# A four-layer transformer kernel: a new order of steps around the routed experts, writes of results moved to another queue, and register loads moved behind a wait

## The chip, the cores and the metric

The kernel runs on one core of a Trainium2 chip. A core has five engines that run their own instruction streams: TensorE (PE in the profile, with its weight loads as PEld), VectorE (DVE), ScalarE (ACT), GpSimd (POOL) and SyncE (SP). They meet at semaphores, and sixteen DMA engines move data for them. The metric is the time of one execution on the device, in microseconds.

## The reference

Sixteen blocks of 128 rows with 256 features go through four layers; each layer is a cross attention and a feed-forward part, each behind a LayerNorm and added to x:

```
x = x + L0_xattn(ln(x), ctx); x = x + L0_ffn(ln(x))
x = x + L1_xattn(ln(x), ctx); x = x + L1_ffn(ln(x))     # L1_ffn: routed experts
x = x + L2_xattn(ln(x), ctx); x = x + L2_ffn(ln(x))
x = x + L3_xattn(ln(x), ctx); x = x + L3_ffn(ln(x))
```

The change lies around L1_ffn, in which each row goes to two of seven experts and to one shared expert:

```
gate = xt @ Wr + br
_, ids = top_k(gate + gate_bias, 2)
probs  = softmax(gate where chosen, else -inf)
u  = xt @ Wup[e] + bup[e]                     # per expert e
g  = silu(u @ Wgate[e] + bgate[e]) * u
eo = g @ Wdown[e] + bdown[e]
out = sum_e probs[:, e] * eo[e]
su = xt @ Wsu + bsu;  sg = silu(su @ Wsg + bsg) * su
out = out + sg @ Wsd + bsd
```

and its follower L2_xattn, with 16 heads of 16 features, a LayerNorm over each head's queries and keys, and 16 further context rows with projections of their own. All of it is fp32 in and out.

## The kernel before

**Stages.** The program numbers its stages: 0 and 1 are layer 0, 2 is L1_xattn, 3 the router of L1_ffn, 8 its routed tiles, 9 its shared expert with the gathering and combining of results, 4 and 5 layer 2, 6 and 7 layer 3. x stays in SBUF through the whole program; each stage runs over 16 blocks of 128 rows.

**The order.** Each engine walks through a string of letters (`ORDER`, one string each for T = PE, V = DVE, A = ACT, G = POOL). A letter stands for one step of a stage (`STEPS` names the steps and the engines that take part), and `timetable()` gives each letter's next occurrence the next block. So the strings alone decide what stands behind what on an engine. A step waits on semaphores for its inputs and for its PSUM bank; a wait that an engine has passed once is not repeated. SP has no string: it issues weights and tiles in the order of its code.

**Router (3).** Per block: `lnA`, `lnB`, `xT` (normalise, transpose), `r1` (scores on PE, top two on DVE, exponential on ACT), `r2` (weights of the two), `pT`, `acc`, `rk` (running counts), `sc` (POOL scatters the block's normalised rows into the DRAM buffer `rows_in`, sorted by expert). After the last block `tab` makes the table of 38 tiles: first row and expert of each.

**Tiles (8).** For tile t, SP reads its first row into a register and loads 128 rows (`tile_in`, six buffers). Step `cp` reads the tile's expert number into a register (`value_load`, on ACT at L1440 and on DVE at L2009) and copies that expert's weights from the SBUF block that holds all of them into one of two buffers: ACT the up matrix, DVE gate and down (L2012). PE then transposes (`tT`, L1088), and multiplies with up (L1096), gate (L1105) and down (L1112, L1113). DVE adds biases and multiplies by u (L2019, L2024), ACT does the activation and evicts the result into one of three buffers. POOL writes it to the DRAM buffer `rows_out` (L2362).

**Shared expert and combination (9).** Steps `up`, `ga`, `dn` on PE (L1123, L1131, L1138) run for the 16 blocks; they stand in the order among the router's steps, the tiles and the start of stage 4. When all of `rows_out` is written, POOL gathers per block two sets of rows (`gt`, two indirect DMAs at L2356, ring of six buffers), and DVE adds them to x with their weights (`cmb`, L2048 and L2050). A block's `cmb` must be done before its `lnA` of stage 4, in which POOL takes a part (L2269).

**Stage 4.** Its weights come by eleven DMAs (L711 to L722). `cw` (DVE, L1624 to L1666, once) subtracts head means from them. PE's first step is `vp`, the values of the context (L851); it waits for `cw` and for stage 4's `init` on POOL.

## Time and profile before

| | us |
|---|---|
| median of three runs | 2449.25 |
| the three runs | 2446.4, 2449.25, 2453.49 |
| profiled execution | 2446.4 |
| its span | 2444.5 |
| PE busy | 2304.7 (94%) |
| DVE busy | 1689.5 (69%) |
| ACT busy | 1178.2 (48%) |
| POOL busy | 444.0 (18%) |

The span runs from the first instruction to the last; the device's time is 1.9 us more. "Busy" is the time in which an engine executes; waiting at a semaphore isn't counted. In timelines a bracket behind an instruction gives how long its engine had been idle, and what released it.

The stretches of this case within the span: PE's last output projection of stage 2 ends at 1107.3, the first tile's transpose starts at 1145.9, the last tile's down ends at 1273.3, stage 4's `vp` starts at 1287.7 and its first score matmul at 1304.7, and its last output ends at 1537.4.

### The profile page before, as it was taken

The page shows a single profiled execution, that of the slowest core. Times are in us where ns is not written, and L with a number is a line of the kernel's source. Part 1 is how long each engine was busy: PE and PEld are TensorE (multiplying, and loading weights), DVE is VectorE, ACT ScalarE, POOL GpSimd, SP SyncE. Part 2 cuts the span into 40 slices and gives each one's busy share as a digit, 9 for nine tenths or more (in the row PEclk, how much of TensorE's full clock was granted, in tenths as well). Part 3 has the DMA queues.
Part 4 walks back from the last instruction along what each step waited for, and adds up shares of the span by engine and source line. Part 5 has one row for each costly group of instructions (what it writes and reads, how often), then busy time and mean ns, then how long its engine had stood idle before and what let it go on. Part 6 is the DMA issues. An engine that isn't in the chain of part 4 may idle for free.

```text
span 2444.5 us, 43996 instructions
## 1 busy us (share of the span) xinstructions
PE 2304.7 (94%) x16327; PEld 1811.9 (74%) x16327; DVE 1689.5 (69%) x4612; ACT 1178.2 (48%) x3093; POOL 444.0 (18%) x514
## 2 busy tenths in 40 slices
PE   4899999999999999997998999999999999999987
PEld 3666999999888888886997887886666666665554
DVE  5997887876355555546447888326776777869997
ACT  3677877677433333332643444114555555553211
POOL 2220100000011111002127842001222222220000
PEclk9999999999999999998998999999999999999999
DMA  9200300000210000002211110301000000000000
GB/s 342 68 2 2 104 1 1 1 1 1 80 33 10 10 9 10 10 9 65 83 61 29 34 36 1 121 1 52 1 1 1 1 1 1 1 1 3 13 9 11
DMA packets 52976, 74.88 MB, mean 31 GB/s; under 512 B 4666, under 2 KB 45644, under 8 KB 51740
## 3 DMA queue, kind: packets, MB, share of 16 engines
q1 hardware_dynamic: 47868, 58.69, 7.3%
q0 software_dynamic: 4896, 13.38, 1.7%
q8 instruction: 131, 2.15, 0.4%
q14 instruction: 81, 0.66, 0.1%
HBM read 45.32 MB, written 26.74 MB: 29 GB/s over the span
## 4 chain that ended last, share of the span: by engine, by line
PE 68%; DVE 18%; ACT 7%; issue 4%; POOL 2%; SPq 1%; DMA 0%; POOLq 0%; DVEq 0%; ACTq 0%
PE pb L972 5%; PE pb L1041 5%; PE pb L964 4%; PE pb L978 4%; PE pb L885 4%; PE pb L1156 4%; PE pb L1010 4%; ACT workA L1525 3%; PE pb L1033 3%; PE pb L911 2%; PE pb L1021 2%; PE pb L1164 2%; PE pb L1227 1%; PE pb L1096 1%; ACT workA L1420 1%
## 5 line engine op out<-in xcount | busy, mean ns | idle before, releaser
L2269 POOL TENSOR_TENSOR sm<-sm,neghalf 128x1 f32<-128x1 f32 x128 | 72.8, 569 | 1047.2 <-DVE sm L1603 1047.0
L1390 ACT ACTIVATE areaB<-i128h,workB 128x128 f16<-128x128 f16 x512 | 156.2, 393 | 4.3 <-DVE workB L1828 4.2
L1525 ACT ACTIVATE workA<-pb,workA 128x128 f32<-128x128 f32 x256 | 114.0, 457 | 81.6 <-DVE workA L2137 81.6
L1618 DVE TENSOR_TENSOR x<-x,pb 128x256 f32<-128x256 f32 x112 | 46.8, 418 | 137.5 <-PE pb L1164 53.4
L1347 ACT ACTIVATE areaA<-pb 128x512 f32<-128x512 f32 x192 | 105.3, 600 | 62.9 <-PE pb L885 62.6
L885 PE MATMUL pb<-workA 32*128 32x128 f16 (+2 forms) x2048 | 121.7, 256 | 14.1 <-DVE workA L1713 4.6
L1227 PE MATMUL pb<-areaA,workA 128*128 128x256 f32 x512 | 122.7, 383 | 10.6 <-DVE workA L2149 9.9
L885 PEld LDWEIGHTS pb<-workA 32*128 32x128 f16 (+2 forms) x2048 | 92.4, 144 | 47.8 <-issue 27.6
L1010 PE MATMUL pb<-xT,areaA 128*128 128x128 f32 x1024 | 125.1, 279 | 0.0
L1010 PEld LDWEIGHTS pb<-xT,areaA 128*128 128x128 f32 x1024 | 122.6, 196 | 2.0 <-issue 1.3
L964 PE MATMUL pb<-areaB 128*128 128x128 f32 x1024 | 123.4, 277 | 0.6 <-ACT workB L1380 0.6
L1227 PEld LDWEIGHTS pb<-areaA,workA 128*128 128x128 f32 x512 | 94.5, 191 | 35.3 <-issue 12.1
L1041 PE MATMUL pb<-areaA,workA 128*128 128x256 f32 x512 | 120.0, 381 | 0.0
L964 PEld LDWEIGHTS pb<-areaB 128*128 128x128 f32 x1024 | 118.1, 192 | 1.6 <-ACT workB L1380 0.8
L2338 POOL TENSOR_TENSOR workA<-workA,neghalf 128x4 f32<-128x4 f32 x64 | 64.5, 1010 | 270.0 <-DVE workA L2116 270.0
L978 PE MATMUL pb<-areaB,workB 128*128 128x256 f32 x512 | 113.5, 380 | 0.0
L1041 PEld LDWEIGHTS pb<-areaA,workA 128*128 128x128 f32 x512 | 94.4, 190 | 17.4 <-issue 6.7
L1420 ACT ACTIVATE workA<-pb,workA 128x128 f32<-128x128 f32 x256 | 90.6, 369 | 32.0 <-DVE workA L1860 28.7
L978 PEld LDWEIGHTS pb<-areaB,workB 128*128 128x128 f32 x512 | 96.1, 190 | 13.0 <-issue 0.5
L1156 PE MATMUL pb<-workB,areaB 128*128 128x128 f32 (+1 forms) x768 | 97.6, 280 | 0.0
L1412 ACT COPY workA<-pb 128x512 f32<-128x512 f32 x64 | 38.0, 594 | 122.8 <-PE pb L1010 122.7
L1156 PEld LDWEIGHTS pb<-workB,areaB 128*128 128x128 f32 (+1 forms) x768 | 86.6, 179 | 10.1 <-issue 5.8
(412 smaller groups left out, 5915.9 us busy)
## 6 DMA issues: line engine op xcount, KB each, us to landing
rows_in<-areaB SPq DMA_DIRECT2D x7, 2048.0 KB, 17.5
areaA<-rows_in SPq DMA_DIRECT2D x38, 128.0 KB, 2.0
rows_out<-areaA POOLq DMA_DIRECT2D x38, 128.0 KB, 2.0
areaA<-in_L_xattn_Wo SPq DMA_DIRECT2D x2, 2048.0 KB, 19.4
areaB<-in_edT SPq DMA_DIRECT2D x1, 2048.0 KB, 9.5
areaB<-in_L_ffn_e_up SPq DMA_DIRECT2D x1, 2048.0 KB, 15.5
areaA<-in_wq1T SPq DMA_DIRECT2D x1, 2048.0 KB, 8.3
areaA<-in_L_xattn_Wq SPq DMA_DIRECT2D x1, 2048.0 KB, 7.6
```

Source lines behind the costliest of these rows:

```text
L885: m = eng.matmul(p[i][:, j * 128:(j + 1) * 128], one, two, start=True, stop=True)
L964: m = eng.matmul(p[:, e * 128:(e + 1) * 128], w.ed[:, k, (4 * c + e) * 128:(4 * c + e + 1) * 128], xT[:, k, :], start=(k == 0), stop=(k == 1))
L972: m = eng.matmul(p[:, g * 64:(g + 1) * 64], u.B[c % 2][:, g, :], u.Am[c % 2][:, g, :], start=True, stop=True)
L978: m = eng.matmul(p[:, 0:256], G[:, e, :], w.eu[:, e, :], start=(e == 0), stop=(e == 15))
L1010: m = eng.matmul(p[:, h * 128:(h + 1) * 128], w.wq[:, 4 * c + h, k], xT[:, k, :], start=(k == 0), stop=(k == 1))
L1041: m = eng.matmul(p[:, 0:256], u.OT[i][:, h], w.wo[:, 4 * c + h], start=(c == 0 and h == 0), stop=(c == 3 and h == 3))
L1156: m = eng.matmul(p[0:M, m_ * 128:(m_ + 1) * 128], wm[:, k, mt * 128:mt * 128 + M], xT[:, k, :], start=(k == 0), stop=(k == 1))
L1227: m = eng.matmul(p[:, 0:256], u.OT[i][:, h], w.wo[:, 4 * c + h], start=(c == 0 and h == 0), stop=(c == 3 and h == 3))
L1347: eng.activation(u.P[n % RP], bank(s, tag, b, c // 2)[:, :], ACT.Exp, scale=1.0 / math.sqrt(hd)).then_inc(freed(s, tag, b, c // 2)[0], 1)
L1390: m = eng.activation(u.far[:, g], i128h[:, :], ACT.Square, bias=u.at[b % 2][:, 1, 8 * c + g:8 * c + g + 1])
L1420: m = eng.activation(u.P[i][:, h], p[:, h * 128:(h + 1) * 128], ACT.Exp, accum_out=u.den[i][:, h:h + 1], bias=u.nm[i][:, h:h + 1])
L1525: m = eng.activation(u.P[i][:, h], p[:, h * 128:(h + 1) * 128], ACT.Exp, accum_out=u.den[i][:, h:h + 1], bias=u.nb[i][:, h:h + 1], scale=u ...
```

## The change

Four things are edited.

1. The four order strings, from the end of stage 1's and stage 2's work to stage 4, and a pair of letters in stage 6 (T and V).
2. The writes of `rows_out` go from POOL to SP: step `dn` of stage 8 loses its "G", POOL's function `tiles` goes, and SP's loop gets `tile_out`.
3. Stage 4's weights (eleven DMAs) are issued behind the load of tile 6, no longer ahead of the tiles.
4. In `cp`, on ACT and DVE, `value_load` stands behind the wait for the end of the tile two earlier.

```diff
@@ STEPS
-    8: (("cp", 1, "AV"), ("tT", 1, "TA"), ("up", 1, "TV"), ("ga", 1, "TAV"), ("dn", 1, "TAG")),
+    8: (("cp", 1, "AV"), ("tT", 1, "TA"), ("up", 1, "TV"), ("ga", 1, "TAV"), ("dn", 1, "TA")),
@@ ORDER, one line of "V" out of some hundred changed ones
-        "eafhOkgkbekhkfgkkefhkkrgkkihkkQgrakkbihQkkatbQkkaQkkbeifarrbeQQfQQgeathfigkkberkkfrgrahtbhikkrQekkftgrkkirkkhtgrkkre"
+        "QQieafbiQeafQgebfhakgkbekkhfagkkefhbkkrgkkiahkkbQekgkfrikkrhagbtFhkkiekkfrekkfirgktkrarrgbeFFhfrkthtkrkkirergtkhkfta"
@@ SP
+            def tile_out(t):
+                d.wait_ge(*freed(8, "dn", t))
+                eng.dma_start(rows_out[128 * t:128 * (t + 1), :], u8.y[t % 3]).then_inc(S[f"m_y{t % 3}"], 16)
+
             def tiles():
                 for b in range(NB - 4, NB):
                     d.wait_ge(*scattered(b))
                 d.wait_ge(S["m_tab"], 1)
-                for t in range(TILES):
-                    tile_in(t)
+                for t in range(TILES + 8):
+                    if t < TILES:
+                        tile_in(t)
+                    if t == 6:
+                        weights(4)
+                    if t >= 8:
+                        tile_out(t - 8)
@@
             for k in range(FIRST + 1, LAST + 1):
-                weights(k)
                 if k == 4:
                     tiles()
+                else:
+                    weights(k)
@@ ACT, cp
                     a.wait_ge(S["m_tab"], 1)
-                    e = eng.value_load(u3.tei[0:1, b:b + 1], min_val=0, max_val=EXPERTS - 1)
                     if b >= 2:
                         a.wait_ge(*full(8, "u", b - 2))
+                    e = eng.value_load(u3.tei[0:1, b:b + 1], min_val=0, max_val=EXPERTS - 1)
                     eng.copy(u.w[b % 2][:, 0:1], w3.all[:, bass.ds(e, 1), 0]).then_inc(S["m_wa"], 1)
@@ DVE, cp
                     v.wait_ge(S["m_tab"], 2)
-                    e = eng.value_load(u3.tei[0:1, b:b + 1], min_val=0, max_val=EXPERTS - 1)
                     if b >= 2:
                         v.wait_ge(*full(8, "dn", b - 2))
+                    e = eng.value_load(u3.tei[0:1, b:b + 1], min_val=0, max_val=EXPERTS - 1)
                     eng.tensor_copy(u.w[b % 2][:, 1:3].unsqueeze(1), w3.all[:, bass.ds(e, 1), 1:3]).then_inc(S["m_wv"], 1)
@@ POOL
-            def tiles(step, b, c):
-                g.wait_ge(*freed(8, "dn", b))
-                eng.dma_start(rows_out[128 * b:128 * (b + 1), :], u8.y[b % 3]).then_inc(S[f"m_y{b % 3}"], 16)
```

Lines of the new kernel lie ten further than those of the old one from stage 0's code on, and 12 further for `cp` on DVE before its wait. What the new strings do is seen in the instructions, below; "waits" names the semaphores.

**First place: DVE, block 15 of the router, between the max subtraction and the softmax sum.** Before, `cw` stands there (L1624 to L1666, areaA is stage 4's weights):

```order
L1909 TENSOR_SCALAR workB<-workB 128x7 [waits dve_own]
L1624 TENSOR_REDUCE areaA<-areaA 128x32 [waits w_in4]
L1626 TENSOR_SCALAR areaA<-areaA 128x32 [waits dve_own]
L1628 TENSOR_TENSOR areaA<-areaA 128x512 [waits dve_own]
...
L1666 TENSOR_SCALAR areaA<-areaA,cst 128x256 x2
L1912 TENSOR_REDUCE workB<-workB 128x1 [waits m_exp]
L1914 RECIPROCAL workB<-workB 128x1 [waits dve_own]
```

Now the same place has one multiplication of the shared expert (L2049):

```order
L1919 TENSOR_SCALAR workB<-workB 128x7 [waits dve_own]
L2049 TENSOR_TENSOR workB<-workB 128x256 [waits bank_free4]
L1922 TENSOR_REDUCE workB<-workB 128x1 [waits m_exp]
L1924 RECIPROCAL workB<-workB 128x1 [waits dve_own]
L1928 MEMSET workB 128x1 [waits dve_own]
```

`cw`, sixteen instructions, has left the router.

**Second place: DVE in the tiles.** bank_full5 and 6 are PSUM banks that PE fills with down's result; bank_full1 to 4 those of up and gate. Before, the register load (TENSOR_LOAD and two ISA instructions) is ahead of the wait for down:

```order
L2024 TENSOR_TENSOR areaA<-areaA 128x256 [waits bank_free3,bank_free1]
L2009 TENSOR_LOAD workB
L2009 ISA x2
L2012 ISA [waits bank_full6]
L2012 COPY areaA<-areaB 128x1024
```

Now the wait stands on the load:

```order
L2034 TENSOR_TENSOR areaA<-areaA 128x256 [waits bank_free4,bank_free2]
L2029 TENSOR_TENSOR areaA<-pb,workB 128x256 [waits m_gm,bank_full4,bank_full1]
L2021 TENSOR_LOAD workB [waits bank_full6]
L2021 ISA x2
L2022 ISA
L2022 COPY areaA<-areaB 128x1024
```

The load, its two register instructions and the copy are all behind down's end now.

**Third place: PE in the tiles, as it is now.** L1098 and L1099 are the transpose, L1106 up, L1115 gate, L1122 and L1123 down:

```order
L1122 MATMUL pb<-areaA 128x256 [waits bank_free5,m_gm]
L1123 MATMUL pb<-areaA 128x256
L1098 MATMUL pb<-cst,areaA 128x128 [waits bank_free0,m_x1]
L1099 MATMUL pb<-cst,areaA 128x128
L1106 MATMUL pb<-areaA 128x128 [waits bank_free2,m_wa]
L1106 MATMUL pb<-areaA 128x128 x3
L1115 MATMUL pb<-areaA 128x128 [waits bank_free3,m_wv]
L1115 MATMUL pb<-areaA 128x128 x3
```

m_wv is DVE's copy of gate and down; here it waits for the down that stands at the head of these rows, and a transpose and an up lie between.

**Fourth place: DVE ahead of stage 4, as it is now.** m_g3 to m_g5 and m_g0 are the gathers of a block; L2058 and L2060 are `cmb`:

```order
L2058 SCALAR_TENSOR_TENSOR x<-areaA,workB,x 128x256 [waits bank_free6,m_g4]
L2060 SCALAR_TENSOR_TENSOR x<-areaA,workB,x 128x256 [waits dve_own]
L1634 TENSOR_REDUCE areaA<-areaA 128x32 [waits w_in4]
...
L1676 TENSOR_SCALAR areaA<-areaA,cst 128x256 x2
L2058 SCALAR_TENSOR_TENSOR x<-areaA,workB,x 128x256 [waits bank_free7,m_g5]
L2060 SCALAR_TENSOR_TENSOR x<-areaA,workB,x 128x256 [waits dve_own]
L2058 SCALAR_TENSOR_TENSOR x<-workB,x 128x256 [waits bank_free6,m_g0]
L2060 SCALAR_TENSOR_TENSOR x<-workB,x 128x256 [waits dve_own]
L1735 SCALAR_TENSOR_TENSOR workA<-pb,cst,areaA 128x16x16 [waits bank_full0,l2_init]
```

The first pair is block 10's. Before, two combinations stood ahead of stage 4's first eviction (L1725) beyond block 0's, and `cw` none.

**POOL.** Before, three blocks are gathered, and the others between stage 4's steps. Now POOL's part is:

```order
L2366 DMA workB<-rows_out,workB 128x256 [waits m_y2,m_out,m_y1,m_y0]
L2366 DMA workB<-rows_out,workB 128x256 x5
L2279 TENSOR_TENSOR sm<-sm,neghalf 128x1 [waits ln_var0]
L2366 DMA areaA<-rows_out,workB 128x256 x2
L2279 TENSOR_TENSOR sm<-sm,neghalf 128x1 [waits ln_var0]
L2366 DMA areaA<-rows_out,workB 128x256 x2
```

This goes on to block 5 with one L2279 per block (four in all), and then without one to block 11: 22 gathers for blocks 0 to 10. The shared expert's steps for blocks 9 to 15 stand behind the last tile on PE, with the down steps of blocks 8 to 15.

## Rows read from the trace of the kernel before

**Rows 1.** The page, section 1: busy us (share of the span) xinstructions.
```profile
PE 2304.7 (94%) x16327; PEld 1811.9 (74%) x16327; DVE 1689.5 (69%) x4612; ACT 1178.2 (48%) x3093; POOL 444.0 (18%) x514
```

**Rows 2.** Stretches: length, busy us of each engine (xcount), clock, DMA share, GB/s.
```profile
1107.30:1145.90 38.60, 24.41 (x163) 21.25 (x161) 26.39 (x89) 9.94 (x21) 9.81 (x18) 0.84 0.19 52
1145.90:1273.30 127.40, 125.08 (x902) 116.17 (x903) 61.48 (x133) 71.83 (x193) 20.05 (x37) 0.98 0.24 77
1273.30:1287.70 14.40, 12.94 (x103) 12.25 (x101) 9.05 (x25) 3.77 (x12) 9.41 (x12) 1.00 0.26 82
1287.70:1304.70 17.00, 13.46 (x68) 10.33 (x68) 14.96 (x39) 4.29 (x9) 15.83 (x12) 1.00 0.08 25
1304.70:1537.40 232.70, 224.14 (x2231) 187.48 (x2232) 187.29 (x526) 97.99 (x178) 120.41 (x78) 0.96 0.08 23
```

**Rows 3.** PE timeline: start, us, instruction, [idle before <-releaser].
```profile
1131.02 0.80 PE L1138 MATMUL pb<-areaB,workB 128*128 128x256 f32 x1 [6.45 <-DVE workB L2039]
...
1137.53 0.39 PE L1081 MATMUL pb<-workB,cst 128*128 128x8 f32 x2
...
1145.90 0.47 PE L1088 MATMUL pb<-cst,areaA 128*128 128x128 f32 x1 [6.91 <-DMA areaA<-rows_in]
```

**Rows 4.** DVE timeline, router block 15; columns as in rows 3.
```profile
1122.84 0.68 DVE L1624 TENSOR_REDUCE areaA<-areaA 128x32 f32<-128x512 f32 x1
...
1129.60 0.15 DVE L1912 TENSOR_REDUCE workB<-workB 128x1 f32<-128x7 f32 x1
```

**Rows 5.** PE timeline, two tiles in the middle of the tile stage.
```profile
1184.31 0.60 PE L1112 MATMUL pb<-areaA 128*128 128x256 f32 x2
...
1185.18 0.27 PE L1088 MATMUL pb<-cst,areaA 128*128 128x128 f32 x1
...
1185.40 1.06 PE L1096 MATMUL pb<-areaA 128*128 128x128 f32 x8
1186.29 1.11 PE L1105 MATMUL pb<-areaA 128*128 128x128 f32 x8
```

**Rows 6.** DVE timeline there: the copy of a tile's gate and down weights.
```profile
1185.50 0.69 DVE L2012 COPY areaA<-areaB 128x1024 f32 x1 [2.04 <-PE pb L1113]
```

**Rows 7.** Line 2009: durations ns min/median/max, first and last start.
```profile
L2009 DVEq TENSOR_LOAD <-workB x38: 297/304/544, 1147.8 to 1266.1; - x38
...
L2009 DVEq SEQ_ASSERT  x38: 23/23/35, 1148.7 to 1266.7; - x38
```

**Rows 8.** POOL timeline, the last write of results and the first gathers.
```profile
1274.04 0.54 POOL L2362 DMA_DIRECT2D rows_out<-areaA  x1 [1.19 <-ACT areaA L1464]
1276.80 1.02 POOL L2356 DMA_INDIRECT workB<-rows_out,workB  x1 [2.21 <-DMA rows_out<-areaA]
1278.12 0.97 POOL L2356 DMA_INDIRECT workB<-rows_out,workB  x1 [0.30 <-issue]
...
1283.16 0.95 POOL L2356 DMA_INDIRECT workB<-rows_out,workB  x1 [0.30 <-issue]
...
1285.00 1.11 POOL L2356 DMA_INDIRECT areaA<-rows_out,workB  x1 [0.19 <-issue]
```

**Rows 9.** The page, section 6: KB each, us from issue to landing.
```profile
areaA<-rows_in SPq DMA_DIRECT2D x38, 128.0 KB, 2.0
```

**Rows 10.** SP timeline: first and last of eleven weight issues, first tile loads.
```profile
1107.97 0.37 SPq L711 DMA_DIRECT2D areaA<-in_L_xattn_Wq  x1
...
1112.73 0.42 SPq L722 DMA_DIRECT2D areaA<-in_nwc  x1
1143.93 1.49 SPq L764 DMA_DIRECT2D areaA<-rows_in  x2
```

**Rows 11.** DVE timeline, the combination of block 0 and what follows.
```profile
1280.86 0.49 DVE L2048 SCALAR_TENSOR_TENSOR x<-workB,x 128x256 f32<-128x256 f32 x1 [0.87 <-DMA workB<-rows_out,workB]
...
1281.90 0.43 DVE L1599 BATCH_NORM_STATS2 sm<-x 128x6 f32<-128x256 f32 x1
```

**Rows 12.** PE timeline, the first step of stage 4.
```profile
1287.74 0.67 PE L851 MATMUL pb<-areaA,ctxT 128*128 128x256 f32 x2 [0.57 <-POOL workA L2308]
```

More of the change, by code:

```diff
@@ L83 @@
[L83 to L86 removed]
+        "nnnkhplrnhnlsnhlnnpnjhlnrnksplnCnlnDplnnCElrnnFpslnnnDnFpCFrEsFDNFNCEFDNFENFFNFNPNNFFkPkNNFkNFCNFDNFCENFDNFCEDNEkPkN"
@@ new lines @@
+        "NkFFkFPkNNFlFNCNDFCEFDFCENNPNNPFFFDNNFCENNFFFPDNNFCENNFFFPDNNFCENNFFFPDNNFCENNFFFPDNNFCENNFFFPDNNFCENNcFFFPDcNENlNcF"
+        "FNlFlFPNNlFNFNlFlFPNlNFNmFNFPNNdPeddeegdcdheegidhegidhegidhecigddheCgiDhegdFhGegHihiigdcheCgihDgihgFdGhHeiigdheCiDdg"
+        "dFhGeHeicgdhegihdiegdheCgihDgihdFiGeHdcdeegddheecigddheCgiDhegdFhGegHihiigdcheCgihDgihgFdGhHeiigdheCiDdgdFhGeHeicgdh"
+        "egihdiegdheCgihDgihdFiGeHdcdeegddheecigddheCgiDhegdFhGegHihiigdcheCgihDgihgFdGhHeiigdheCiDdgdFhGeHeicgdhegihdiegdheC"
@@ new lines @@
+        "gihDgihdFiGeHdcdeegddheeigddheCgiDhegdFhGegHihiigddheeCgiDhgdiFhGeHgihgdheigdheCgihDgihiFiGMHMNNMOONCMODNMMONFNFGOHM"
+        "OJNbbcbcbbddceebcdcbdebccdebcbcdbecbedbcdebcOdbecedbcdebcdbecedbcdebcdbecedcbdecbdebcdecbdecbdebcdcecbdebdbecdecbdec"
+        "bdbecdecbdecbdbecdecbdecbdecdecdedeMMdeNNdeOeMONMMONNMOMONcNMMcNNcOOOOidcidcdhcdjjchljmdoomhojoqcljimhojomdoojlqcqmi"
+        "jmsholooomtooimhjdqqjoodcjslqimjtoomlFqFFFFqdmhoooosmsqoojthtqqcjiqdsjlthsmtoomijqdjoojlcqmiloomshqmoodtmijhcdjqoooo"
@@ new lines @@
+        "NNGHIMNMNPJKGOOHIJMMNNOOPKBMNMNABABGOOHAIMMNNOOJPKMNMNGHIPJOOKBMNMNOOABMNMNGHIOOJPKMNMNOOABMNMNGHIOOJPKMNMNOOABMNMNG"
+        "HIOOJPKMNMNOOABMNMNGHIOOJPKMNMNOOAaBMNMNGHIOOJPKbiiiMNMNOOMNaMNGHIOOJPKbaMNObMNOaMNGHMNIJOOKbPMNMNOOMNMNOOPMNOMNOMNm"
+        "MNOOPOOPefeeffabheefhefhefhaebiiiiABfhefDhEeFfhGeHfhiiiiABafhebfhDEhFGhHefiiiiABhefDEFhGeHefafbhefhiiiiAeBfhefhDEhFG"
+        "eHafbeeffheaebiiiiABfhefDhEeFfhGeHfhiiiiABafhebfhDEhFGhHefiiiiABhefDEFhGeHefafbhefhiiiiAeBfhefhDEhFGeHafbeeffheaebii"
@@ L2373, in gpsimd_program @@
                     experts(step, b, c)
-                elif s == 8:
-                    tiles(step, b, c)
                 elif s == 2:
```

63 lines of the change are left out of this document (25 added, 38 removed).

## The prediction

> **What bounds the kernel now.** I read the page's first line first [rows 1]: TensorE (PE) is busy 94% of the span, VectorE (DVE) 69%. So a change pays only where PE idles, and costs wherever it makes PE wait. The table of stretches comes next [rows 2]: the five stretches in which the order changes. PE is busy 24.4 of 38.6 us between the last output projection of stage 2 and the first expert tile, 125.1 of 127.4 in the tiles, 12.9 of 14.4 and 13.5 of 17.0 at the handoff to stage 4, and 224.1 of 232.7 in stage 4 itself. Only the first has much to win. PE's timeline there [rows 3] has two long holes: 6.45 us before 1131.02 and 6.91 before 1145.90. I count from the profiled execution: 2446.4 us, of which 2444.5 is the span and 1.9 lies around it. The median of the three runs is 2449.25, 2.85 higher.
>
> **The change, part by part.**
>
> *Router tail.* The first hole ends on a DVE step queued behind `cw`, the centring of stage 4's weights. It runs from 1122.84 to the next reduce at 1129.60 [rows 4]: 6.8 us, and the product that PE waits for (L2039) comes behind both. In the new order `cw` isn't in that chain, and the product (L2049) directly follows the max subtraction. So the route table is ready 6.8 us sooner. The second hole stays: from the table's matmul at 1137.53 to the first tile's transpose at 1145.90 are 8.4 us of DVE, SP and DMA chain, and PE has as little to fill it with. Value: -7. Bounds: 0 (another input is late there) and -13.4 (both holes, 6.45 + 6.91).
>
> *Tiles.* PE needs per tile 0.22 (transpose), 0.89 (up), 0.89 (gate, as many matmuls) and 0.87 (down), from the differences of the starts in [rows 5]: 2.87, or 109.1 for 38. The other shared-expert work in the stretch was ten steps of 0.88, 8.8; now six, 5.3: -3.5, which comes back after the tiles. The order now has two shapes. Weight buffers are two, so gate(b) waits for DVE's copy(b), and that for the end of down(b-2). Before, the copy starts at 1185.50 and takes 0.69 [rows 6], and gate starts at 1186.29, 1.11 after down gave way at 1185.18 [rows 5]: the 0.22 + 0.89 of other PE work between them just hides it. Now the register load of the expert number comes behind that wait. It is a load (0.30), register arithmetic and a check (0.02) [rows 7]; from the load's last start (1266.1) to the check's (1266.7) it is 0.6. Before, it ran while DVE waited (the copies' engine waits for down, 2.04 us in [rows 6]). So the need grows from 1.11 to 1.7. In the new order, PE's work between down(b-2) and gate(b) is 1.11 for 14 tiles, 0.89 for five, 0.22 and 0 for one each; the others have 1.76 or more. Stalls: 14 x 0.6 + 5 x 0.8 + 1.5 + 1.7 = 15.6, of which 12.6 (21 x 0.6) is the moved load and 3 the tighter order. Before, the stretch took 127.4 for 117.9 of work (109.1 + 8.8); of these 9.5 I let 3 go, as the new order leaves gate and down further apart where they stood close. Stage: -3.5 + 15.6 - 3 = +9. Bounds: -3.5 if the load costs nothing (-3.5 + 3 - 3), +15 if every tile with 1.76 also stalls by 0.35. I take +9, since in [rows 5, 6] copy and gate touch without a gap (1185.50 + 0.69 is 1186.19, gate starts 0.10 later).
>
> The Trainium skill ("DMA: Bandwidth & Descriptors", section "Latency and other measured facts") gives a register load a floor of about 600 ns; [rows 7] has 297 to 304, so the trace doesn't agree. By the page each of the 21 stalls would be 0.3 longer, the sum 6 us higher.
>
> *Writes from SP.* The 38 writes of results leave POOL and stand on SP, tile t-8's behind the load of tile t. POOL spent 0.54 on each [rows 8] and was otherwise idle (20.0 of 127.4 busy), so nothing comes back there. A load now waits behind a write of eight tiles earlier, which is long evicted. A load of the same size from SP lands 2.0 after its issue [rows 9]; from POOL's last write to the first gather it was 2.76 (1274.04 to 1276.80, [rows 8]), landing and the gather's own start. So the first gather stays about as far behind the last tile. Value 0, bounds -0.5 and +3.
>
> *Weights of stage 4.* Eleven issues, from 1107.97 to the end at 1113.15 [rows 10], 5.2 us, now stand between the loads of tiles 6 and 7. Load 6 is issued once tile 0 is transposed; from there 0.75 for it (two loads took 1.49), 5.2, 0.75 for load 7 and 2.0 to landing are 8.7, and a few us more behind the weights' own data. Tile 7 is due on PE 7 x 2.87 = 20 us after tile 0, or 16 as transposes run ahead. 0, bounds 0 and +2.
>
> *Handoff.* This is the term that decides. PE's first step of stage 4 (vp, L861) waits for `cw`, which on DVE stands behind the combination of block 10, and that for the 22nd gather. Gathers follow each other by 1.25 to 1.32 us (1276.80 to 1278.12, 1.32, [rows 8]; most later ones at 1.25); one with a LayerNorm helper in between takes 1.84 (1283.16 to 1285.00), 0.6 more. From the first gather: 21 x 1.26 + 4 x 0.6 = 28.9 to the start of the 22nd; 2.74 from a block's last gather to its combination (1278.12 to 1280.86, [rows 8, 11]); 1.0 for its two operations (to 1281.90); 6.8 for `cw`; 0.2 to PE. Sum 39.6. The first gather starts 3.4 after the last tile (1273.3 in [rows 2], 1276.80), so vp starts 43.0 after the tiles; before 14.4 (1273.3 to 1287.74, [rows 2, 12]). +28.6. PE has 22 shared steps x 0.88 = 19.4 to fill it with, and then stands still for about 20 us. Bounds: +22 (helpers free, `cw` half as long) and +31.
>
> *Stage 4.* Before, 17.0 + 232.7 = 249.7 from vp to its last output [rows 2]. In the 17.0, the first LayerNorm and transposes are late; now x and xn of four blocks are ready: -2.3, and 1.7 more since qk of a block is done sooner. Ten combinations of 1.0 and four LayerNorm halves (some 3 us) leave DVE's part in the stage, and the gathers POOL's. DVE had 187.3 busy of 232.7, PE 224.1, so it was not DVE that filled the stage; what can come back is PE's 8.6 idle us, and I take 6. Sum -10. Bounds 0 and -19 (every microsecond of DVE counts).
>
> Sum: -7 + 9 + 28.6 - 10 = +20.6, on the profiled execution 2467.0, against the median 2469.8. A check by PE's idle time: -6.5 in the router, +12.6 in tiles, about +20 in the handoff (43.0 - 19.4 less the 5.0 idle of before [rows 2] gives 18.6), -4 to -6 in stage 4: +19 to +21.
>
> **The rivals.**
>
> *A, the forecast*: +20.6, 2469.8.
>
> *B, no change.* The load in the tile loop hides after all (DVE's instruction stream reads it ahead of the wait, or PE has more slack than its starts show), -12, and stage 4 gives 7 more because combinations no longer sit in its DVE chains. 20.6 - 19 = +1.6, 2451. For it: DVE was 80% busy in stage 4 (187.3 of 232.7) with long chains. Against: a register load written behind a wait runs behind it, and PE's slack is one of 8.6 us.
>
> *C, faster.* DVE, not PE, paces all of these stages. Then all 19 us of DVE work that leave stage 4 come back rather than 10 (-9), the tile load hides (-12), both router holes go (-6.4), and the helpers among the gathers cost nothing (-2.4): 20.6 - 29.8 = -9, 2440. For it: PE at 94% [rows 1] is a busy share, and waits of under 0.1 between its instructions would not show in it. Against: PE's starts follow each other without a gap in [rows 5]. It decides from 20 us of gain outside the handoff on.
>
> *D, worse.* The tile loop is set by the copies: ScalarE's copy of up(b) has its load moved behind a wait in the same way, and a stalled gate delays gate's activation, down and so the next copy. 0.35 more on each of 38 tiles (+13): 2483. For it: ACT is busy 71.8 of 127.4 only, but in the chain of each tile. Against: up(b) has a whole gate and down ahead of it. That the writes on SP hold up loads would be of the same size.
>
> That the change doesn't do what it says would be B's first half alone: +8, inside A's range.
>
> **How the numbers follow.** A 0.72, B 0.08, C 0.07, D 0.13. A's own range: terms' bounds about half used, 2457 to 2482. The whole range reaches down to B and up to D: 2450 to 2486. About 0.3% (7.3 us) is what a measurement of this kernel tells from no change: faster (C) 0.07, same (B and the low end of A) 0.09, slower 0.84.
>
> **What would show it.** The first tile's transpose about 7 us earlier than 1145.90, with no `cw` on DVE before it. In the tiles, PE idle of some 13 us in pieces of 0.6 to 0.8 before L1115, released by DVE's copy L2022, whose start trails down's end by 0.6 more. A hole of about 20 us on PE before L861, with DVE waiting for gathers, 22 of them before `cw`, and a lower granted clock just behind it. Stage 4 shorter by about 10. The forecast is wrong if that hole is under 10 us, if L2022's load is not in the path, or if stage 4 shortens by over 15.

## The result and the profile after

The changed kernel takes 2489.48 us (median of four runs, 2486.1 to 2492.1), the kernel before 2449.9 beside it: 39.6 us more, a ratio of 1.0161 with a 95% interval of 1.0141 to 1.0180. It is slower, as forecast, but by nearly twice the forecast 20.6, and lies above the range that was given (2450 to 2486).

The profiled execution took 2500.7, 11 above the median, with a mean granted clock of 0.975 where the other four had 0.977 to 0.981. So its stages add up to +54.3 against the profiled execution before, not to +39.6; where that matters it is said. Every length of a stage below is from one profiled execution. Page, section 1, of the changed kernel (against [rows 1]):

```profile
PE 2320.0 (93%) x16327; PEld 1815.3 (73%) x16327; DVE 1694.9 (68%) x4612; ACT 1178.0 (47%) x3095; POOL 425.3 (17%) x476
```

The same stretches as in [rows 2], and stage 2 ahead of them (length, busy us of each engine, clock, DMA share, GB/s):

```profile
640.00:1097.10 457.10, 455.56 (x2868) 372.39 (x2867) 238.51 (x764) 175.17 (x683) 45.58 (x55) 1.00 0.07 23
1097.10:1131.00 33.90, 24.21 (x168) 21.27 (x167) 21.29 (x79) 9.83 (x21) 11.22 (x20) 0.97 0.06 20
1131.00:1280.40 149.40, 128.85 (x878) 113.78 (x879) 60.72 (x129) 67.51 (x191) 0.00 (x0) 0.97 0.25 77
1280.40:1328.00 47.60, 21.66 (x150) 18.93 (x148) 32.22 (x77) 5.75 (x18) 34.02 (x40) 0.81 0.27 80
1328.00:1591.70 263.70, 250.68 (x2285) 206.70 (x2286) 190.34 (x533) 104.23 (x185) 111.46 (x60) 0.91 0.04 11
```

Stage 2 of the kernel before, which I had not looked at:

```profile
640.00:1107.50 467.50, 466.57 (x2859) 382.63 (x2858) 236.63 (x765) 171.12 (x665) 45.33 (x57) 0.97 0.07 23
```

The span less PE's busy time grew from 139.8 to 178.9 us. From the landmarks on PE (profiled executions, us):

| part | before | after | difference | forecast |
|---|---|---|---|---|
| to the end of stage 2 | 1107.5 | 1097.1 | -10.4 | 0 |
| to the first tile | 38.4 | 33.9 | -4.5 | -7 |
| tiles | 127.4 | 149.4 | +22.0 | +9 |
| last tile to vp | 14.4 | 47.7 | +33.3 | +28.6 |
| vp to stage 4's last output | 249.6 | 263.7 | +14.1 | -10 |
| stages 5 to 7 | 904.5 | 904.5 | 0 | 0 |

The end of stage 2 is measured from the span's start. Counted from the first of the router's score products, which stand among stage 2's steps (687.4 before, 690.0 after), to the stage's end, it is 420.1 before and 407.1 after, 13.0 less; 12 of these are the time at half clock, 27 us before and 3.4 after (from the granted clock in steps of 2 us), and the rest is a little less work between the two marks.

Every part but the last is off: the first was not in the forecast, stage 4 has the wrong sign, and the tiles and the handoff lie above their bounds (+15 and +31). The hole in front of vp is there as forecast, 21 us. The other stretches had to be taken apart by experiments.

In the tiles, two groups of the changed kernel hold nearly all of PE's waits (gate, and the transposes; busy us, mean ns, idle before <-releasers):

```profile
L1115 PE MATMUL pb<-areaA 128*128 128x128 f32 x304 | 42.2, 283 | 5.7 <-DVE areaA L2022 5.6
...
L1098 PE MATMUL pb<-cst,areaA 128*128 128x128 f32 x38 | 12.2, 322 | 20.7 <-DMA areaA<-rows_in 17.7 <-ACT areaA L1458 2.8
```

and the same two before:

```profile
L1105 PE MATMUL pb<-areaA 128*128 128x128 f32 x304 | 40.6, 277 | 0.0
...
L1088 PE MATMUL pb<-cst,areaA 128*128 128x128 f32 x38 | 11.3, 298 | 8.8 <-DMA areaA<-rows_in 7.5 <-ACT areaA L1448 1.1
```

The transposes waited 17.7 us for their loads, the gates 5.6 for DVE's copy. Of the 17.7, 6.8 lie ahead of the first tile and so outside the stage (6.9 of the 7.5 before); within the stage the waits for loads are 10.9 us against 0.6. I had put 15.6 on the copy and nothing on the loads. How a load comes to be late shows in three timelines of one tile. ScalarE's eviction of a down result (L1474) stands behind a weight copy (L1453) that waits for a later tile's up:

```profile
1199.03 0.62 ACT L1453 COPY areaA<-areaB 128x512 f32 x1 [2.24 <-PE pb L1106]
1199.56 0.36 ACT L1474 COPY areaA<-pb 128x256 f32<-128x256 f32 x1
```

SP waits for that eviction with the write (L768), and the load of tile 24 (L764) stands behind the write; the load ahead of it had been issued six us before:

```profile
1194.92 0.34 SPq L764 DMA_DIRECT2D areaA<-rows_in  x1
1199.95 0.33 SPq L768 DMA_DIRECT2D rows_out<-areaA  x1
1201.04 0.34 SPq L764 DMA_DIRECT2D areaA<-rows_in  x1
```

PE gets the tile 2.9 us after the issue:

```profile
1203.91 0.33 PE L1098 MATMUL pb<-cst,areaA 128*128 128x128 f32 x1 [1.85 <-DMA areaA<-rows_in]
```

Before, an eviction was done 1.4 to 1.5 us after the start of its down, in all 38 tiles; in the changed kernel it is some 4 to 10 us from the tenth tile to about the thirtieth. Before, loads were issued 12 to 21 us ahead of their transposes from tile 8 on; in the changed kernel it is 2.0 to 4 us from tile 15 on. The queue's own waits say the same, total us, times and longest:

```profile
SPq L768 <- ACT areaA L1474: 89.4, 33, 6.7
```

Before, SP waited in the tiles only for the buffers of its loads.

### The profile page after: what moved, and what is told of

Read it like the earlier page. It is cut to its first block, busy times and chain, and to the rows that moved or that the text cites. A ratio compares the mean times of both kernels' runs of the same rounds, so it can differ in the third digit from the quotient of the medians.

```text
span 2498.9 us, 43992 instructions
## 1 busy us (share of the span) xinstructions
PE 2320.0 (93%) x16327; PEld 1815.3 (73%) x16327; DVE 1694.9 (68%) x4612; ACT 1178.0 (47%) x3095; POOL 425.3 (17%) x476
## 4 chain that ended last, share of the span: by engine, by line
PE 67%; DVE 18%; ACT 6%; issue 4%; POOL 2%; DMA 2%; SPq 1%; ACTq 0%; another core or an unknown queue 0%; DVEq 0%; POOLq 0%
PE pb L982 4%; PE pb L1051 4%; PE pb L974 4%; PE pb L1020 4%; PE pb L988 4%; PE pb L895 4%; PE pb L1166 4%; PE pb L1031 3%; ACT workA L1535 3%; PE pb L921 2%; PE pb L1043 2%; PE pb L1174 2%; PE pb L1237 2%; PE pb L1229 1%; PE pb L1199 1%
## 5 line engine op out<-in xcount | busy, mean ns | idle before, releaser
L2279 POOL TENSOR_TENSOR sm<-sm,neghalf 128x1 f32<-128x1 f32 x128 | 72.9, 569 | 1006.6 <-DVE sm L1613 1006.4
L1051 PEld LDWEIGHTS pb<-areaA,workA 128*128 128x128 f32 x512 | 93.2, 190 | 12.9 <-issue 2.4
L2330 POOL TENSOR_TENSOR areaA<-areaA,neghalf 128x32 f32<-128x32 f32 x16 | 87.2, 5450 | 39.1 <-DVE areaA L1691 39.1
```

Of the source, the lines that this page charges most:

```text
L1051: m = eng.matmul(p[:, 0:256], u.OT[i][:, h], w.wo[:, 4 * c + h], start=(c == 0 and h == 0), stop=(c == 3 and h == 3))
```

## The experiments

All are variants of the two kernels; "old code" is that of before, "new order" the strings of the change. Each time is a median beside runs of the kernel before on the same chip (2448.1 to 2452.5 in the batches). Stage lengths are from profiled executions.

**Writes back on POOL** (`w_pool`):

```diff
-    8: (... ("dn", 1, "TA")),
+    8: (... ("dn", 1, "TAG")),
-                    if t >= 8:
-                        tile_out(t - 8)
+            def tiles(step, b, c):          # POOL, ahead of the gathers
+                g.wait_ge(*freed(8, "dn", b))
+                eng.dma_start(rows_out[...], u8.y[b % 3])...
```

> The changed kernel, with one part undone: the 38 writes of results go through POOL again (step dn of stage 8 has its G, the writes stand ahead of the first gather), SP only loads tiles. Everything else, the new order and the moved register loads too, is as in the changed kernel. Theory S (the writes on SP close a loop: the load of tile t+1 stands behind the write of tile t-8, that behind ScalarE's eviction, which in the new order stands behind the transposes of later tiles, which wait for their loads): PE's wait for tile loads in the tile stage, 17.7 us in the changed kernel's trace against 7.5 before, falls to about 8, evictions trail their down by 1.4 again, and the tile stage (first transpose to last down, 149.4) falls by 12 to 20; the kernel takes about 2473. Rival L (the moved register load sets the pace of the tiles): the stage shortens by under 4 us, 2486 to 2490.

2487.3 us (ratio 1.0153, 1.0126 to 1.0180); tile stage 142.6, 6.8 shorter. The load waits went to their old value, and the copy waits doubled:

```profile
L1108 PE MATMUL pb<-areaA 128*128 128x128 f32 x304 | 42.4, 283 | 12.5 <-DVE areaA L2015 12.5
...
L1091 PE MATMUL pb<-cst,areaA 128*128 128x128 f32 x38 | 11.2, 296 | 10.8 <-DMA areaA<-rows_in 6.9 <-ACT areaA L1451 3.8
```

Theory S was right about the waits for loads and wrong in what they are worth: another wait stood right behind. (All of the 6.9 is the first tile's.) It was wrong about the evictions too: they did not return to 1.4 us but were done 5 to 8 us after the start of their down in the same tiles. So the writes on SP are not what makes them late. The medians differ by 2.2 us only, which the two intervals don't tell from nothing, nor from the stage's 6.8.

**Register loads ahead of the wait again** (`vload`):

```diff
-                    if b >= 2:
-                        v.wait_ge(*full(8, "dn", b - 2))
                     e = eng.value_load(u3.tei[0:1, b:b + 1], ...)
+                    if b >= 2:
+                        v.wait_ge(*full(8, "dn", b - 2))
```

(the same on ScalarE)

> The changed kernel with its register loads ahead of the wait again, on ACT and DVE; the rest as changed. Theory S: the tiles are paced by the loads through SP, so the register load matters little: 0 to -4 us against the changed kernel's 2489.5. Rival L (my forecast's term): -12 or more, 2477 or less.

2475.5 us (1.0095, 1.0078 to 1.0112), tile stage 137.9. The rival held: the load is worth 14 us by the medians, 11.5 in the stage. PE's wait for the copy is gone, that for the loads is unchanged:

```profile
L1115 PE MATMUL pb<-areaA 128*128 128x128 f32 x304 | 40.7, 277 | 1.0 <-DVE areaA L2022 0.9
...
L1098 PE MATMUL pb<-cst,areaA 128*128 128x128 f32 x38 | 12.0, 316 | 19.1 <-DMA areaA<-rows_in 17.3 <-ACT areaA L1458 1.7
```

So PE's idle time had not told what each part is worth: undoing the part with 10.9 us of waits within the stage gave 6.8, undoing the part with 5.6 gave 11.5. (TensorE's weight loads, PEld, which overlap its matmuls, waited another 9.4 us for the same copy, which the line of the matmuls doesn't show.)

**Both undone** (`both_loops`):

> The changed kernel with both parts undone: register loads ahead of the wait and the writes on POOL. Its tile stage took 149.4, with the writes undone alone 142.6, with the loads undone alone 137.9. Theory P (two loops of nearly the same length, either of which holds up the tiles): the stage falls below both, to 126 to 132, so by 18 to 23, and the kernel takes 2467 to 2472. Rival Q (only the register load counts, the writes cost nothing once it is gone): 136 to 138, 2474 to 2477.

2470.4 us (1.0083, 1.0058 to 1.0107), tile stage 127.1, as long as before:

```profile
L1108 PE MATMUL pb<-areaA 128*128 128x128 f32 x304 | 41.7, 281 | 2.2 <-DVE areaA L2015 1.9
...
L1091 PE MATMUL pb<-cst,areaA 128*128 128x128 f32 x38 | 11.1, 292 | 8.9 <-DMA areaA<-rows_in 7.5 <-ACT areaA L1451 1.3
```

Theory P. The two parts together cost 22.3 (149.4 to 127.1), alone 6.8 and 11.5: two loops of nearly the same length, each of which hides part of the other. The medians say 19.1 for both, 2.2 and 14.0 alone. The evictions were still done 3 to 7 us after the start of their down here, so it is the new order of ScalarE that makes them late. With the register loads already ahead, undoing the writes gave 10.8 (137.9 to 127.1), and that is what PE's waits for loads in the stage were there (17.3 less the first tile's 6.8): with one loop left, the waits do tell.

The stage is as long as before, but with less in it: four steps of the shared expert, 3.5 us by the forecast, stand behind it now. So the new order of the tiles costs some 3 us by itself, of which the gates' wait for the copy, 1.9 against 0.0 before, is a part. This run still issues stage 4's weights behind tile 6, so that part of the change costs nothing that shows here.

**The same two parts put into the old kernel** (`b_sp`, `b_vload`), with the old order throughout; the edits are those above, the other way round.

> The kernel before with its old order and one part of the change: the writes of results on SP, tile t-8's behind the load of tile t; weights of stage 4 and register loads as before. In the old order ScalarE evicts a tile's result 1.4 us after its down, and loads were issued 12 to 20 us ahead of their transpose. Theory S2 (the write on SP costs only where evictions are late, as in the new order): tile stage 127.4 plus 0 to 3, time within 3 us of before. Rival S1 (the coupling costs by itself): loads land just in time in every tile, PE waits for them by 5 or more, 2455 and above. Also a second profile of stage 2 in the old order: if its half-clock stretches (28 us in all before, none in five profiles with the new order) come with the order, they are there again.

2453.1 us (1.0008, 0.9991 to 1.0025), tile stage 126.9: the writes on SP cost nothing where evictions are done 1.4 us after the start of down. Of the two orders tried, they are bad only with the new one.

> The kernel before with its old order and the register loads behind the wait, on ACT and DVE; nothing else. Undoing this in the changed kernel gave 14 us. By the forecast's way of counting: gate(b) needs 1.7 after down(b-2), and the old order gives it 1.11 in one tile of two and 1.76 in the other, so 19 x 0.6 = 11.4, tile stage 139, 2461. Rival: in the old order the load hides in DVE's wait for something else, 0 to 4, 2450 to 2453. Stage 2 as in the run before this one.

2461.2 us (1.0036, 1.0020 to 1.0052), tile stage 134.6. By the median +8.8 (beside 2452.5), by the stage +7.2; the count gave 11.4. The rival, 0 to 4, falls, and the way of counting is right in kind and too high by 2.6 to 4.2. That the forecast 2461 was met to the microsecond is luck: it was counted from a kernel before of 2450.

**New order up to the last tile, old order behind it** (`old_tail`; the code as changed). The strings are cut at each engine's last step of stage 8, and the steps that are missing follow in the old order.

> The changed kernel's order up to the last tile on every engine, and behind it what is left in the old order: cw stands right behind the tiles on DVE, three blocks are combined ahead of stage 4 and the others inside it, the gathers between stage 4's helpers. Theory H (vp waits for cw, cw for the 22nd gather): the hole of 21 us before vp goes, vp starts about 14 to 16 us after the last tile, not 47.6, and stage 4 takes about 250 us rather than 263.7, as its long stretch at half clock was run into by the hole and the new order: in all -35 to -45 us, 2445 to 2455. Rival D (stage 4 had taken its gain from fewer steps, and only the hole is bad): stage 4 becomes longer by 5 to 10 and the gain is 20 to 25, 2465 to 2470.

2465.3 us (1.0060, 1.0035 to 1.0084), 24 less than the changed kernel, but its runs lie between 2456.5 and 2479.7, and the profiled one (2479.0) is at the slow end. Handoff 24.8 against 47.7: 22.9 us of the handoff are the tail's order. Stage 4 took 267 there, with 65 us at half clock; so this run bears out neither theory's figure for stage 4. The other executions but one were at 2456.5 to 2465.7 with a mean clock of 0.983 to 0.987, against 0.976 in the profiled one.

**New order up to the first tile only** (`new_head`; old code, old order from the tiles on).

> The kernel before, with the new order only up to the first tile (stages 1 to 3), and the old order from there on; no edit of the code. In the two traces the new order reached the end of stage 2 at 1097.1 against 1107.5 and went from there to the first tile in 33.9 against 38.4. Theory O (both come from the order: the short half-clock stretches in stage 2, 13 to 15 us in all in the trace of before, come with the old order's rhythm): -12 to -17 against before, 2433 to 2438. Rival R (the clock in stage 2 differs from execution to execution, whatever the order; only cw's move in the router is the order's): -4 to -7, 2443 to 2446.

2438.9 us (0.9967, 0.9943 to 0.9991): 10.8 faster than the kernel before. Stage 2 ended at 1096.8, as in the changed kernel, at nearly full clock:

```profile
640.00:1096.80 456.80, 455.26 (x2867) 372.20 (x2865) 238.44 (x764) 174.97 (x682) 45.69 (x55) 1.00 0.07 23
```

In the seven profiles up to then with the new order stage 2 had one half-clock stretch of 3.4 us (four profiles) or none (three); in the three with the old it had seven or eight, 24 to 27 us in all. From the first of the router's score products to the stage's end it is 406 to 407 us with the new order and 418 to 420 with the old, whatever the execution. So this gain is the order's and not an accident. The router's stretch was 34.4 (38.4 before). But 5.8 us were lost again in the tiles (133.2 against 127.4), where PE stood 3.6 us for the copies behind cw and was longer at half clock (11 us against 5).

**r1 moved by one step in the old order** (`r1_sc2`). On PE, in 13 blocks:

```diff
-  pt(b+1,0)  r1(b)  sc(b+1,2)  pv(b+1,0)
+  pt(b+1,0)  sc(b+1,2)  r1(b)  pv(b+1,0)
```

> The kernel before, with one step of PE moved: in 13 of 16 blocks the router's scores r1 (products of 7 columns) stand directly between pt and sc of stage 2; here r1 stands behind that sc. Nothing else. In the three profiles with the old order eight or nine half-clock stretches follow r1 in stage 2, 28 us in all; in the seven with the new order there are none. Theory W1 (it is r1 in a row with other light steps that brings the clock down): the stretches become fewer or shorter, stage 2 (467.5) falls by up to 10, 2440 to 2448. Rival W2 (it is the rhythm of the whole stage, r1's place in it matters little): 25 us or more at half clock as before, 2449 to 2453.

2459.3 us (1.0048, 1.0030 to 1.0065), but see stage 2:

```profile
640.00:1115.10 475.10, 463.68 (x2862) 380.39 (x2862) 235.56 (x766) 170.00 (x665) 45.30 (x57) 0.99 0.07 23
```

The half-clock time fell from 27 us in eight stretches to 14 in four, and PE's idle time there rose from 0.9 to 11.4, since the router's later steps come later. So W1 is right in part: half of the falls hang on r1's place among the other steps, if they don't hang on the new idle time, which came with the same edit. What the new order does for the other half isn't shown. The time was lost in another way, so no sum of mine for it holds.

**cw ahead of all combinations** (`cw_first`; the rest as changed):

```diff
   # DVE's order behind the last tile
-  ... cmb(10)  cw  cmb(11)  cmb(12)  vp(0) ...
+  cw  ... cmb(10)  cmb(11)  cmb(12)  vp(0) ...
```

> The changed kernel with one step moved on DVE: cw stands right behind the last tile's step, ahead of all combinations, which stay ahead of stage 4's first eviction. Theory H1 (what holds stage 4 is the row of gathers and combinations on POOL and DVE; cw only adds its own 6.8 us to it): vp itself starts some 20 us earlier, but PE then waits for DVE's eviction of it, the first score matmul comes 6 to 8 us earlier, and the kernel takes 2481 to 2484. Rival H2 (cw is what holds it, the combinations behind it are quick): the first score matmul comes 15 or more earlier, 2475 or less.

2493.4 us (1.0162, 1.0132 to 1.0191): no gain. The hole in front of vp shrank to 11.4, and had another releaser:

```profile
1320.78 1.19 PE L861 MATMUL pb<-areaA,ctxT 128*128 128x256 f32 x2 [11.37 <-POOL workA L2318]
```

L2318 is POOL's copy of a context block, which vp waits for too (`l2_cm`). It stands in `lnB`, behind 24 gathers. The handoff became 42.1, 5.6 shorter; the step on DVE in the middle of the shared expert's work cost PE 4.3 us at 1280 and the rest later. H2 falls: cw alone is not what holds stage 4. H1 is right that the row of gathers holds it, but not in how: vp came 5.6 us sooner after the last tile and not 20, as it waits for the gathers itself, and the first score matmul only 0.7 (66.9 against 67.6).

**Old order up to the last tile, new order behind it** (`new_tail2`; old code, cw in the router).

> The old code with the old order up to the last tile and the new order behind it (the old order had cw in the router, so cw is not in the tail). Theory H1 (vp is held by the gathers as such: its context copy, l2_cm, stands behind 24 of them on POOL, so it would wait without cw too): a hole of 12 to 16 us ahead of vp, handoff 36 to 41 us against 14.4; stage 4 at 255 to 264, with the hole of 2.3 us some 120 us into it and a half-clock stretch behind that; in all 2474 to 2486. Rival H2 (cw was all): handoff under 25, 2460 or less. Rival C (the low clock in stage 4 came from the thin tile stage ahead): stage 4 takes 250 or less.

2483.3 us (1.0142, 1.0123 to 1.0160). Handoff 36.4 and stage 4 261.8, as H1 has it; the hole ahead of vp is 11.4, and C falls, as the tiles were the old ones. The same releaser:

```profile
1314.96 0.76 PE L851 MATMUL pb<-areaA,ctxT 128*128 128x256 f32 x1 [11.35 <-POOL workA L2308]
```

So the tail alone costs 35 us, 22 of them in the handoff and 12 in stage 4.

**The half-clock stretch in stage 4.** In each of the six profiles with the new tail up to here PE has a hole of 2.3 us some 120 us into the stage and falls to half clock with it, in the changed kernel until 1480:

```profile
1451.86 0.70 PE L843 MATMUL pb<-areaA,xT 128*128 128x256 f32 x2 [2.33 <-POOL workA L2318]
```

```profile
1452.00:1480.00 28.00, 28.00 (x172) 23.29 (x173) 16.82 (x40) 8.40 (x15) 7.93 (x6) 0.52 0.00 1
```

In four of the others this stretch was 17 to 27 us too; in `w_pool`, behind the same hole, it was 3.4, and after some 3 us at full clock another 10. The releaser is again POOL's context copy, which stood behind a power (L2330) of 5.4 us:

```profile
1444.89 5.42 POOL L2330 TENSOR_TENSOR areaA<-areaA,neghalf 128x32 f32<-128x32 f32 x1 [7.87 <-DVE areaA L1691]
1450.27 1.53 POOL L2318 COPY workA<-ctxT 128x16 f32<-128x16 f32 x1
```

`swap` puts the copy (lnB of block 10) ahead of that power (nb of block 9) on POOL; nothing else.

> The changed kernel with two steps of POOL exchanged in stage 4: lnB of block 10, whose context copy PE's qk of block 10 waits for, now stands ahead of nb of block 9 (the power of 5.4 us) instead of behind it. Theory G (the hole of 2.3 us, which is 120 us into stage 4 in all five profiles with the new tail, comes from that power, and the 20 to 28 us at half clock that start with it come from the hole): the hole falls under 1 us, no half clock follows at that place, stage 4 falls by 10 to 14 (263.7 to about 251), the kernel takes 2476 to 2480. Rival G2 (the half clock comes at that place without the hole as well, by the thin work around it): the hole goes, the clock still falls, 2486 to 2488. Rival G3 (the copy waits for something else, or block 9's normalisation becomes the late one): the hole is moved, not closed, 2488 to 2492.

2487.3 us (1.0144, 1.0127 to 1.0161): G3, though the time is below its range. The hole moved, and 14 us at half clock follow it: PE now waits for DVE, which is in a 5.8 us piece of the next stage's weight preparation (tp).

```profile
1449.72 1.16 PE L895 MATMUL pb<-workA 16*128 16x128 f32 x16 [2.47 <-DVE workA L1726]
```

`tp_late` moves the last three such pieces to near the end of the stage.

> The kernel of the run swap, with three steps of DVE moved as well: the last three pieces of the ternary weights (tp, 5.8 us of DVE each), which the new order has about 115, 130 and 175 us into stage 4, stand near its end, where the old order has them. In swap the hole was closed in front of qk and opened again behind the first of these pieces, 2.5 and 2.9 us, and the half-clock stretch was there too. Theory G (the hole brings the half clock): no hole of over 1.3 us in the middle of stage 4, no half-clock stretch there, the stage falls from 258.8 to 246 to 250, the kernel takes 2474 to 2479. Rival G2 (the clock falls there without a hole too): the stage at 255 or more, over 2483. Rival G4 (the pieces do as much harm at the end): the middle is clean, but holes and low clock near the end, 2483 to 2488.

2506.7 us (1.0229, 1.0215 to 1.0243), worse by 19 than `swap`. The hole in the middle is 3.7 us, and DVE waits in it for POOL's next step behind the same power:

```profile
1452.36 0.93 PE L921 MATMUL pb<-areaA,workA 128*64 128x128 f32 x8 [3.71 <-DVE workA L1735]
```

```profile
1451.11 0.41 DVE L1623 TENSOR_SCALAR xn<-x,sm 128x256 f32<-128x256 f32 x1 [4.41 <-POOL sm L2279]
```

and there are holes of 3.2 and 4.9 us near the end, each with a half-clock stretch behind it. Three attempts, three holes, and a fall of the clock with each: this fits that the hole brings the low clock. No run with the new tail had the middle of the stage without a hole. The kernel before has none of over 1.3 us between 1322 and 1470, and was at full clock there; but its order differs in much else, so the cause is not shown. Two things in the traces speak against the hole alone: in stage 2 the clock fell with PE idle for under 1 us in all, and in the changed kernel's tiles it stayed full behind holes of 1.85 and 1.53 us (1203.91 and 1269.38), while it fell behind one of 1.97 (1220.52).

**Towards a better version.** `head_cw2` is `new_head` with cw moved on DVE behind the second weight copy; `tiles_cw2` also takes the new order of the tiles, with the old code.

> The old code with the new order up to the first tile and the old order behind it, as in the run new_head, and cw moved on DVE from ahead of the first weight copy to behind the second (cp of tile 1). In new_head PE stood 3.6 us at 1138 for the copies behind cw. If that hole is cw's: it goes, and 3 to 4 us with it, 2435. If it is only handed on (the bias step of tile 0 now stands behind cw): 0 to -1, 2438.

2438.4 us (0.9956, 0.9942 to 0.9969): 9.7 below before, no gain over `new_head`. PE's hole, which ends at 1141, was 4.8 instead of 3.6 us; it is handed on.

> The old code with the new order up to the last tile, cw behind the second weight copy, and the old order for the rest. It takes the new order's head and tiles without either loop (register loads ahead of the wait, writes on POOL; tile stage 127.1 in both_loops), and not its handoff and stage 4. Sum from the stages measured: 1095 + 34 + 128 + 18 to 20 + 250 to 267 + 134 + 771, and 4 around it: 2434 to 2453, by whether stage 4 takes the old order's 250 or, as in old_tail, 267 with its half-clock stretch of some 44 us. Theory K1 (that stretch is an accident of single executions): 2434 to 2440. Rival K2 (it follows from the new tiles ahead of the old tail): 2446 to 2453.

2440.4 us (0.9981, 0.9963 to 0.9999), at the upper end of K1's range. Stage 4 took 249.9 in the profiled execution, so the stretch of `old_tail` doesn't follow from the tiles ahead. Single executions still come out longer by as much: two of these twelve took 2457.3 and 2458.2 at a mean clock of 0.975, two of seven in `old_tail` 2479 and 2479.7, and one of six in `new_head`, with the old tiles, 2453.8 at 0.977. The tile stage took 133.5 and not 128, as in `new_head` and `head_cw2` (133.2, 133.6): with cw near the tiles, the 4 us that the router had gained by its absence were lost there again. The best versions are the new order up to the first tile with everything else as before, with cw in either place (2438.9 and 2438.4; the intervals don't tell them apart).

## Why the prediction was wrong

The direction was right, and so was its main reason, the handoff. Two steps failed (the writes from SP at 0, stage 4 at -10), the handoff came short, and stage 2 was left out, where a gain hid a part of the errors.

*"0 ... for the writes from SP" failed.* I had looked at when SP's write of tile t-8 is due by the old order, where an eviction is done 1.4 us after the start of its down ("long evicted", says the prediction). In the new one ScalarE's evictions stand behind weight copies and transposes of later tiles, and come 4 to 10 us after it, and a write that waits for one holds the load behind it, which is what those transposes wait for. It is worth 10.8 us with the register loads ahead (137.9 to 127.1), 6.8 with them behind; I gave it 3 at most. I had named the coupling in rival D (2483, the nearest of the four) and not followed it through ScalarE's order.

*The register load was right in size.* 12.6 us forecast; 11.5 in the changed kernel, 15.5 with the writes on POOL (142.6 to 127.1), 7.2 in the old order. The forecast for the stage without the moved load and with free writes was -3.5 (less work) +3 (tighter order) -3 (slack let go); measured it is -0.3 (127.1 against 127.4), so the last two together are wrong by 3: the slack did not go, or the tighter order costs twice as much, or a part of each. Which isn't known.

*The handoff was right in kind, 4.7 short.* The first gather started 2.9 us after the last tile (forecast 3.4), the 22nd 31.3 us after the first (28.9; at one helper POOL waited 2.45 for DVE), its combination 2.7 after it (2.74), and then:

```profile
1317.29 0.48 DVE L2058 SCALAR_TENSOR_TENSOR x<-areaA,workB,x 128x256 f32<-128x256 f32 x1 [1.41 <-DMA areaA<-rows_out,workB]
1317.81 3.04 DVE L2060 SCALAR_TENSOR_TENSOR x<-areaA,workB,x 128x256 f32<-128x256 f32 x1
1320.77 0.67 DVE L1634 TENSOR_REDUCE areaA<-areaA 128x32 f32<-128x512 f32 x1
...
1327.36 0.61 DVE L1676 TENSOR_SCALAR areaA<-areaA,cst 128x256 f32<-128x256 f32 x2
```

The second operation of block 10's combination took 3.04 us, not 0.48, and cw 7.2 (1320.77 to 1327.97; forecast 6.8). PE starts at once:

```profile
1328.07 1.19 PE L861 MATMUL pb<-areaA,ctxT 128*128 128x256 f32 x2 [21.03 <-DVE areaA L1676]
```

The terms that missed are so 2.4 in the row of gathers, 2.5 in this one operation and 0.4 in cw, less 0.6 in the rest. In these 3 us POOL did three additions to x:

```profile
1314.57 0.95 POOL L2366 DMA_INDIRECT areaA<-rows_out,workB  x1 [0.30 <-issue]
...
1317.09 0.96 POOL L2366 DMA_INDIRECT areaA<-rows_out,workB  x1 [0.30 <-issue]
1318.05 0.20 POOL L2318 COPY workA<-ctxT 128x16 f32<-128x16 f32 x1
1318.22 0.72 POOL L2320 TENSOR_TENSOR x<-x,areaA 128x256 f32<-128x256 f32 x1
1318.88 0.19 POOL L2318 COPY workA<-ctxT 128x16 f32<-128x16 f32 x1
1319.03 0.71 POOL L2320 TENSOR_TENSOR x<-x,areaA 128x256 f32<-128x256 f32 x1
...
1319.85 0.71 POOL L2320 TENSOR_TENSOR x<-x,areaA 128x256 f32<-128x256 f32 x1
```

`cw_first` and `new_tail2` have one such operation each as well, 3.02 and 2.90 us, beside the same three additions; the combinations that the traces show elsewhere take 0.47 to 0.63.

The Trainium skill ("SBUF — State Buffer", section "SBUF: two separate sides") says that a VectorE operation with two SBUF inputs and a GpSimd operation that reads SBUF shut each other out of a shared port for their whole length. The rows agree with it in the length (3.04 against 0.48 us). They don't bear out the page's further rule, that whichever starts first has the port: by the recorded starts VectorE's operation was first (1317.81, POOL's copy 1318.05), and it was the one that took longer. No run here took POOL's additions away, so the cause is not shown.

What I missed outright is that cw was one of two gates: the context copy on POOL waited for 24 gathers as well, and without cw 11.4 us of the hole stay (`cw_first`), the handoff 36.4 (`new_tail2`). POOL's helpers stood in my sum as 0.6 us each, not as a gate.

*"Stage 4. ... Sum -10" failed, by its sign.* I let PE's idle time shrink because DVE and POOL had less to do there. It stayed as it was, 12.1 us before and 12.9 after: the gaps are chains between engines, and the new tail has its own. And PE spent some 50 us of the stage at half clock against 20; 30 us more at half speed are some 15 us of work, about all of the +14.1 (PE's busy time grew by 13.1). 22 of the 50 lie within 36 us behind the hole of 21 us, 27 behind the hole of 2.3 us in the middle. The profile before had such stretches too ([rows 2], clock 0.96); I priced holes by their length alone. That the clock took the time is shown by the rows; what brings the clock down in the middle is not. The size belongs to this execution: in `w_pool`, `both_loops` and `swap` stage 4 took 257 to 259, with 34 to 40 us at half clock.

*Stage 2 was left out.* I read the orders from stage 3 on, and called PE saturated before that. It was, at 97% of its clock. The new order brings 10.4 us to the end of that stage, 13.0 counted from the router's first products, which the result hides: the rest of the change costs some 50. Without this gain the error would have been larger.

*The router*: -4.5 instead of -7. The first hole (6.45) is gone; small ones of 0.2 to 0.8 us came in its place. Three other profiles of the old order (`b_sp`, `b_vload`, `r1_sc2`) took 41.5 to 41.7 there, a fourth 38.8, and all with the new one 33.9 to 34.4, so against those the gain is up to 7.8. The second hole is there as forecast:

```profile
1122.92 0.28 PE L1091 MATMUL pb<-workB,cst 128*128 128x8 f32 x2
1123.06 1.14 PE L1141 MATMUL pb<-workB,areaB 128*128 128x128 f32 x8
1131.01 0.47 PE L1098 MATMUL pb<-cst,areaA 128*128 128x128 f32 x1 [6.80 <-DMA areaA<-rows_in]
```

Put together by measured terms: -10 (stage 2), -5 (router), +22 (tiles), +33 (handoff), +14 (stage 4) is +54 for the profiled execution. The medians, 11 lower, had less of it at half clock; which stage had less isn't known, as only one execution has a profile, but stage 4 as `w_pool` has it would be 6.5 of the 11. The check that I made by idle time could not have found the clock: it used the same durations.

## What to carry over

When a queue is given a second kind of work, follow what its new waits depend on in the new order, engine by engine, until the chain ends or closes; a loop costs its whole length per turn and a second loop of equal length hides it, so take both away before judging either. Idle time by releaser says who came last, not what its removal is worth while another wait stands behind it: list all waits of the instruction behind a hole, and leave out idle time that lies ahead of the stage. PE at 99% busy is not yet PE at full speed, so compare the granted clock of the stretches too.

## What the runs showed of the hardware

- The granted clock in a stretch in which PE was idle under 1 us of 467 depended on the order of its steps: 0.97 in stage 2 with seven-column products between transposes and scores (24 to 27 us at half clock), 1.00 with the new order (0 to 3.4 us). Moving that one step left 14 of the 27 us, and opened 11 us of idle time.
- After holes of 2.3 to 3.7 us in the middle of stage 4, TensorE ran at half clock for 14 to 27 us in seven of eight profiles, and for 3.4 and then another 10 in the eighth. Behind holes of 1.85 and 1.53 us in the tiles it did not fall.
- One VectorE operation of 0.48 us took 3.04, 3.02 and 2.90 in three profiles, each time while GpSimd did three additions to x.
